# w2 in two rounded parts, fetched from DRAM slot by slot, in a gated cross-attention block with a mixture of experts

## The reference

```python
x = x + tanh(g_xattn) * xattn(layernorm(x), ctx)
h = layernorm(x).reshape(1024, 256)
probs = softmax(30 * tanh(h @ w_gate / 30)); mask = top2(probs)
for e in range(8):
    out += (silu(h @ w1[e]) * (h @ w3[e])) @ w2[e] * (probs * mask)[:, e:e + 1]
x = x + tanh(g_ffn) * out
```

## Time and profile before

| | us |
|---|---|
| median of 3 runs (685.17 to 686.24) | 685.33 |
| the profiled execution's own time | 686.1 |
| its span | 684.3 |
| PE busy | 641.3 (94%) |
| DVE busy | 599.4 (88%) |
| ACT busy | 550.0 (80%) |
| POOL busy | 466.5 (68%) |
| mean DMA traffic over the span | 55 GB/s |

### The profile page before, as it was taken

How to read it: one execution, slowest core, us unless ns; L and a number is a source line. 1 busy time by engine, 2 the same in 40 slices (tenths; PEclk the granted TensorE clock), 3 DMA queues, 4 the chain that set the end, 5 groups by cost and what they waited for, 6 DMA issues and landing times. The chain is left out here.

```text
span 684.3 us, 14974 instructions
## 1 busy us (share of the span) xinstructions
PE 641.3 (94%) x4573; PEld 588.8 (86%) x4574; DVE 599.4 (88%) x1386; ACT 550.0 (80%) x1927; POOL 466.5 (68%) x646
## 2 busy tenths in 40 slices
PE   1789999999999999999999999999998599999994
PEld 0788999999999999999999999999887588888883
DVE  7998899999999999998999999887799887777771
ACT  5898889899988998998899899988886256666660
POOL 4677786688767778777776886788665525565642
PEclk9999999999999999999999999999999589999998
DMA  7203010100020102002010110100089512333232
GB/s 228 62 2 93 2 32 1 40 25 32 2 62 1 32 2 63 32 1 64 1 32 2 55 43 2 61 3 1 1 300 399 172 39 47 47 54 54 46 46 24
DMA packets 35510, 37.73 MB, mean 55 GB/s; under 512 B 2704, under 2 KB 30352, under 8 KB 35440
## 3 DMA queue, kind: packets, MB, share of 16 engines
q1 hardware_dynamic: 31024, 30.84, 13.5%
q0 software_dynamic: 4416, 6.03, 5.5%
HBM read 31.62 MB, written 5.24 MB: 54 GB/s over the span
## 5 line engine op out<-in xcount | busy, mean ns | idle before, releaser
L1518 POOL TENSOR_SCALAR shared<-shared,rsum 128x256 f32<-128x256 f32 x256 | 143.8, 573 | 52.5 <-DVE rsum L1034 47.6
L717 ACT ACTIVATE shared<-s,nmax 128x256 f32<-128x256 f32 x256 | 122.3, 498 | 23.2 <-DVE nmax L1029 23.0
L1512 POOL TENSOR_TENSOR rstd<-rstd,half 128x7 f32<-128x7 f32 (+1 forms) x64 | 87.8, 1371 | 5.3
L1029 DVE TENSOR_REDUCE nmax<-s 128x2 f32<-128x512 f32 x128 | 86.6, 678 | 1.4 <-PE s L380 1.1
L1039 DVE TENSOR_TENSOR pt_lo<-t,pt_hi 128x512 fp32r<-128x512 f32 x124 | 84.1, 679 | 2.3 <-ACT pt_hi L725 1.3
L725 ACT CAST pt_hi<-t 128x512 fp32r<-128x512 f32 x124 | 73.9, 596 | 10.6 <-PE t L395 7.4
L733 ACT ACTIVATE shared<-route_bank,head_w 128x512 f32<-128x512 f32 (+1 forms) x124 | 81.7, 690 | 0.4 <-PE route_bank L409 0.4
L1024 DVE TENSOR_TENSOR qk_lo<-shared,qk_hi 128x512 fp32r<-128x512 f32 x96 | 77.9, 811 | 2.1 <-POOL qk_hi L1529 1.0
L380 PE MATMUL s<-qk_hi 128*128 128x256 f32 x256 | 77.3, 302 | 2.0 <-DVE qk_lo L1024 1.2
L336 PE MATMUL pj_a<-w_ring,xq 128*128 128x256 f32 x488 | 72.2, 291 | 6.3 <-POOL xq L1594 6.3
L395 PE MATMUL t<-ident,shared 128*128 128x128 f32 x496 | 75.0, 274 | 3.0 <-POOL shared L1518 1.7
(11 more groups left out here) (281 smaller groups left out, 1949.1 us busy)
## 6 DMA issues: line engine op xcount, KB each, us to landing
expert_w<-in_w SPq DMA_DIRECT2D x24, 512.0 KB, 9.3
spare<-in_wT SPq DMA_DIRECT2D x19, 256.0 KB, 3.0
wp_raw<-in_wpT SPq DMA_DIRECT2D x16, 256.0 KB, 2.9
spare<-in_wkvT SPq DMA_DIRECT2D x16, 128.0 KB, 3.3
spare<-in_wT SPq DMA_DIRECT2D x9, 128.0 KB, 3.2
spare<-in_x SPq DMA_DIRECT2D x1, 1024.0 KB, 5.9
x_hat<-acc SPq DMA_DIRECT2D x1, 1024.0 KB, 4.6
out<-spare SPq DMA_DIRECT2D x1, 1024.0 KB, 6.9
```

What stands on the lines that cost most here:

```text
L717: e = act.activation(probs[:, st, h * S:(h + 1) * S], s_bank[st][:, h * S:(h + 1) * S], ACT.Exp, bias=nmax[:, st, h:h + 1], accum_out=psum ...
L1029: dve.tensor_reduce(nmax[:, st, :], s_bank[st][:].rearrange("p (h t) -> p h t", h=2), AX, ALU.max, negate=True).then_inc(max_done, 1)
L1512: pool.tensor_tensor(rstd[:, st, c], rstd[:, st, c], half[:, c], ALU.pow).then_inc(rstd_ready, 1)
L1518: m = pool.tensor_scalar(probs[:, st, c], probs[:, st, c], rsum[:, st, h:h + 1], 1.0, ALU.mult, ALU.mult)
```

## The change

In the attention POOL now makes one pair of instructions in every unit: the two parts of one half of the output weights in b = 0 and b = 3, and the two parts of one half of w2 of expert g in b = 1 and b = 2, in the free half of `wp_ring` (`w2_hi`, `w2_lo`). SP loads w2 into `wp_raw` and stores both parts to a DRAM tensor `w2_parts` of 1 MB per expert. The two pairs of the last expert stand among the hand-written last units. Only w1 and w3 are loaded into `expert_w`.

In the experts SP reads the slot's expert number and fetches 1 MB of parts into one half of `w2_ring`, as soon as the down product two slots earlier is done. ACT rounds `hidT`, DVE makes its rest (`hidden_rest`), and the down product is twelve products of rounded operands. PE turns the hidden rows of slot n right after the rows of slot n + 2, ahead of all products of slot n + 1, and ACT copies `hidT` ahead of rounding w1.

```diff
+            def load_w2(e):
+                sp.dma_start(wp_raw[:], w2[e].rearrange("(j p) h -> p j h", p=P)).then_inc(w2_loaded, 16)
+
+            def store_w2(e):
+                sp.wait_ge(w2_split, 2 * (e + 1))
+                sp.dma_start(w2_parts[e].rearrange("i j p h -> p i j h"), wp_ring[:, (e + 1) % 2].bitcast(F32))\
+                    .then_inc(route.w2_stored, 16)
+
+            for g in range(1, 3):
                 sp.wait_ge(w_ready, g)
                 load_w(g)
-                sp.wait_ge(wp_ready, g)
-                load_wp(g)
-            sp.dma_start(route.gate_w[:], w_gate.rearrange("(k p) e -> p k e", p=P)).then_inc(route.gw_loaded, 16)
-            sp.dma_start(route.table[:], tables).then_inc(route.gw_loaded, 16)
-            sp.wait_ge(w_ready, G)
-            sp.dma_start(x1, x.rearrange("b (s p) h -> p (b s) h", p=P)).then_inc(x_reloaded, 16)
-            def load_expert(e, some=(0, 1, 2)):
+            for g in range(G - 1):
+                sp.wait_ge(wp_ready, g + 1)
+                load_w2(g)
+                if 1 <= g < G - 2:
+                    sp.wait_ge(w_ready, g + 2)
+                    load_w(g + 2)
+                if g == G - 2:
+                    sp.dma_start(route.gate_w[:], w_gate.rearrange("(k p) e -> p k e", p=P)).then_inc(route.gw_loaded, 16)
+                    sp.dma_start(route.table[:], tables).then_inc(route.gw_loaded, 16)
+                    sp.wait_ge(w_ready, G)
+                    sp.dma_start(x1, x.rearrange("b (s p) h -> p (b s) h", p=P)).then_inc(x_reloaded, 16)
+                store_w2(g)
+                load_wp(g + 1)
...
+            load_w2(G - 1)
+            def load_expert(e):
...
+                for i in range(2):
+                    sp.dma_start(at[:, i * n:(i + 1) * n].rearrange("p (k c) -> p k c", k=KT),
+                                 (w1, w3)[i][e].rearrange("(k p) c -> p k c", p=P)).then_inc(route.e_loaded, 16)
 
             sp.wait_ge(pj_done, 4 * U)
-            for e in range(E - 1):
+            for e in range(E):
                 load_expert(e)
-            sp.wait_ge(acc_read, 4 * (G - 1))
-            load_expert(E - 1, (0, 1))
-            sp.wait_ge(tile_out, ST)
-            load_expert(E - 1, (2,))
+            store_w2(G - 1)
...
+                    if g > 0:
+                        wait(route.w2_stored, 16 * g)
...
+            def w2_hi(e, a):
+                if a == 0:
+                    pool.wait_ge(w2_loaded, 16 * (e + 1))
+                    if e > 0:
+                        pool.wait_ge(out_done, 4 * e)
+                n = slice(2 * a, 2 * a + 2)
+                pool.tensor_scalar(wp_ring[:, (e + 1) % 2, 0, n], wp_raw[:, n], 1.0, 1.0, ALU.mult, ALU.mult).then_inc(w2_hi_done, 1)
+
+            def w2_lo(e, a):
+                pool.wait_ge(w2_hi_done, 2 * e + a + 1)
+                n = slice(2 * a, 2 * a + 2)
+                pool.tensor_tensor(wp_ring[:, (e + 1) % 2, 1, n], wp_raw[:, n], wp_ring[:, (e + 1) % 2, 0, n].bitcast(F32),
+                                   ALU.subtract).then_inc(w2_split, 1)
...
-                if prep and b >= 2:
-                    wp_hi(g + 1, 1 - par, b - 2)
-                    wp_lo(g + 1, 1 - par, b - 2)
+                if b == 0:
+                    wp_hi(g, par, 1)
+                    wp_lo(g, par, 1)
+                elif b < 3:
+                    w2_hi(g, b - 1)
+                    w2_lo(g, b - 1)
+                elif prep:
+                    wp_hi(g + 1, 1 - par, 0)
+                    wp_lo(g + 1, 1 - par, 0)
...
             widen(28, 0, 1)
+            w2_hi(G - 1, 0)
+            w2_lo(G - 1, 0)
             power(31, 1)
             heads_hi(30, 2, 2)
             scale_probs(29, 1, 1)
+            w2_hi(G - 1, 1)
+            w2_lo(G - 1, 1)
             scale_probs(30, 0, 0)
...
+            def step(n, par):
+                e = sp.value_load(slot_expert[0:1, bass.ds(n, 1)], min_val=0, max_val=E - 1)
+                if least(n, 2):
+                    sp.wait_ge(y_done, n - 1)
+                sp.dma_start(w2_ring[:, par].bitcast(F32),
+                             w2_parts[bass.ds(e, 1)].rearrange("e i j p h -> p (e i) j h")).then_inc(w2_in[par], 16)
+
+            sp.wait_ge(slots_known, 1)
+            sp.wait_ge(route.w2_stored, 16 * E)
+            steps(sp, step)
             sp.wait_ge(scattered, 16 * SLOTS)
...
             def turn_hidden(n, par):
                 pe.wait_ge(hid_ready, n + 1)
                 if least(n, 1):
-                    pe.wait_ge(ht_ready, n)
+                    pe.wait_ge(ht_split, n)
                 for j in range(IT):
                     m = pe.transpose(ht_bank[:, j * P:(j + 1) * P], hid[:, par, j * P:(j + 1) * P], ident[:])
                 m.then_inc(ht_done, 1)
 
             def down(n, par):
-                e = pe.value_load(slot_expert[0:1, bass.ds(n, 1)], min_val=0, max_val=E - 1)
-                pe.wait_ge(ht_ready, n + 1)
+                pe.wait_ge(ht_split, n + 1)
+                pe.wait_ge(w2_in[par], loads(n, par))
                 if least(n, 2):
                     pe.wait_ge(y_copied, n - 1)
-                for j in range(IT):
-                    m = pe.matmul(y_bank[par][:, 0:H], hidT[:, par, j * P:(j + 1) * P],
-                                  w2_sb[:, bass.ds(e, 1), j, :].rearrange("p e i -> p (e i)"), start=j == 0, stop=j == IT - 1)
+                trio = [(j, l, i) for j in range(IT) for l, i in ((hidT, 0), (hidT, 1), (hidT_lo, 0))]
+                for q, (j, l, i) in enumerate(trio):
+                    m = pe.matmul(y_bank[par][:, 0:H], l[:, par, j * P:(j + 1) * P], w2_ring[:, par, i, j],
+                                  start=q == 0, stop=q == len(trio) - 1)
                 m.then_inc(y_done, 1)
...
                     turn_rows(n + 2, par)
                 more = not isinstance(n, int) or n + 1 < SLOTS
+                turn_hidden(n, par)
                 if more:
                     hidden(n + 1, 1 - par, 0)
-                turn_hidden(n, par)
-                if more:
                     hidden(n + 1, 1 - par, 1)
...
-            act.wait_ge(route.e_loaded, 48 * E)
+            act.wait_ge(route.e_loaded, 32 * E)
...
                     rows_turned(n + 2, par)
-                    weights_high(n + 2, par, (0,))
                 act.wait_ge(ht_done, n + 1)
                 if least(n, 2):
                     act.wait_ge(y_done, n - 1)
                 act.copy(hidT[:, par, :], ht_bank[:]).then_inc(ht_ready, 1)
+                if more:
+                    weights_high(n + 2, par, (0,))
                 if not isinstance(n, int) or n + 1 < SLOTS:
                     silu(n + 1, 1 - par)
...
+            def hidden_rest(n, par):
+                dve.wait_ge(ht_ready, n + 1)
+                dve.tensor_tensor(hidT_lo[:, par, :], ht_bank[:], hidT[:, par, :].bitcast(F32), ALU.subtract).then_inc(ht_split, 1)
+
             def step(n, par):
                 more = not isinstance(n, int) or n + 2 < SLOTS
                 if more:
                     rows_rest(n + 2, par)
                     e = expert_of(n + 2)
+                hidden_rest(n, par)
+                if more:
                     weights_rest(n + 2, par, e, 0)
                 if not isinstance(n, int) or n + 1 < SLOTS:
                     take_hidden(n + 1, 1 - par)
```

More of the change, by code:

```diff
@@ L285, in _ @@
             load_wp(0)
-            for g in range(1, G):
+            def load_w2(e):
[5 more added lines that the diff above has]
+            for g in range(1, 3):
                 sp.wait_ge(w_ready, g)
@@ L1785, in experts @@
         hid = sb("hid", [P, 2, I])
-        hidT = sb("hidT", [P, 2, I])
+        hidT = sb("hidT", [P, 2, I], F32R)
         y_sb = sb("y_sb", [P, 2, H])
@@ L2231, in block_kernel @@
     x_hat = nc.dram_tensor("x_hat", [B * S + P, H], F32).ap()
+    w2_parts = nc.dram_tensor("w2_parts", [w2.shape[0], 2, w2.shape[1] // P, P, H], F32).ap()
     T, E = B * S // P, w1.shape[0]
@@ L2259, in block_kernel @@
         attention(nc, x, ctxT, wT, wkvT, wpT, cols, eye, w_gate, tables, firsts, acc, attn_gate, ident, col, half, spare, row_norm,
-                  route, x_hat, out, expert_w, early, w1, w3, w2)
-        experts(nc, expert_w, early, firsts, out, acc, ident, route, x_hat, slots, w1.shape[2])
+                  route, x_hat, out, expert_w, early, w1, w3, w2, w2_parts)
+        experts(nc, expert_w, early, firsts, out, acc, ident, route, x_hat, slots, w1.shape[2], w2_parts)
 def table_columns(experts, slots, rows):
```

27 lines of the change are left out of this document (13 added, 14 removed).

## The result

The changed kernel takes **702.16 us** (median of four, 699.46 to 704.34) beside 685.25 of the kernel before (685.07 to 686.24): slower, ratio 1.0239, 95% interval 1.0223 to 1.0256. The forecast was 682.5 with a range to 690.5, so it was wrong, and by more than its range.

What follows compares the result with a forecast made beforehand. PE was taken to bound the kernel, at 5.18 us per slot. Terms -6.7 + 1.0 + 0.4 + 1.5 + 1.0 = -2.8 us took the profiled 686.1 to 683.3, median 682.5; range 679.3 to 690.5.

Steps and rivals of the forecast that it cites:

- Point 5: Expert slots: fetching w2's parts brings DMA demand to 5.0 of 4.81 us; scatters settle a little later, costing 1.5 us once.
- Point 1: Down product on PE: twelve products of 0.12 us, 1.44 in all, replace eight passes of 1.73; gain 0.29 us per slot.
- Point 2: Transposes on PE: hidden rows turned directly after the row turns save one switch, 0.08 us per slot; period becomes 4.81.
- Point 4: DVE and ACT in the slots: added work fits, but a new loop of 4.83 us closes; cost 0.4 us for all slots.
- Point 3: Opening of the experts: PE waits for slot 0's hidden rows, and DVE's extra work eats early gains; cost 1.0 us.
- Points 6 and 7: POOL's added pairs: hidden in the attention's units, cost 0; in its hand-written tail, cost 1.0 us, bounds 0 and 2.5.
- Point 8: Kernel's end: the last down product waits 0.7 us longer, but the last scatter waits for a landing anyway; cost 0.
- B: Rival, expert slots: the scatter chain becomes the bound, slower than before; 690.5 us, or 696 at worst; chance 0.28.
- d: Extra time per link between scatters beyond 4.64 us; it costs from 0.17, and 0.8 was seen once.
- the ring: Not forecast, named after the measurement: PE waits for a gather, the gather for a scatter ahead, that scatter for a landing.
- D: Rival, expert slots: fetched parts land after over 8 us and PE waits before the down product; about 692 us; chance 0.05.
- A: Rival, whole kernel: nothing new binds, scatters are undisturbed and the tail absorbs its pairs; -5.7 us, 679.6; chance 0.12.

Runs made afterwards that it cites:

- the exchange: The changed kernel with the gather issued ahead of the scatter on POOL's queue: 696.34 us; the same in the kernel before: 686.29 us.
- the hi-only kernel: The changed kernel with only w2's hi half fetched and eight products for twelve: 688.81 us; also with late first fetches and no lo part made: 692.05 us.
- the half fetch: The changed kernel fetching only the hi half of w2's parts (512 KB) from the third slot on, still twelve products: 685.43 us.
- the last version: The changed kernel with w2's hi part alone, no lo part made, late first fetches, and the gather ahead of the scatter: 682.02 us.

## Why the prediction was wrong

**Point 5 failed.** Its demand was somewhat high: fetch 3.4 us and gathers with scatters 1.6 of a slot's engine time, 5.0 in all; in the stretch that runs at 4.87 us the engines' share is 0.89, which is 4.3. What failed is the step that "a slipping scatter moves out from under the fetch", so that the whole would cost 1.5 us once. The runs show a loss that goes on: links of 118.5 us with the whole fetch and 105.4 with half of it, 13 us in place of 1.5. Its own sign of being wrong, a landing over 4.2 us, came true with a median of 4.6 in 572 to 640 us. The step looked only at the scatter and its own chain. A scatter that slips takes the next gather with it, since both stand in one stream on POOL, and PE waits for that gather. That this way counts is shown by the exchange (5.8 us under the whole fetch, 10 in the hi-only kernel, 0 in the kernel before); that the traffic is what starts it, by the smaller fetches (17 us for the second half of the bytes, nothing for the first). Under the whole fetch it is the smaller part of the loss: with the gather first the links still take 115.3 us, and the waits put that down to scatters that land late and hold y_sb. Why the scatters do not move out from under the fetch is not shown by a run; SP's fetch waits for PE's down product, so a late PE makes a late fetch, and in the trace of the hi-only kernel the scatters settle right behind it.

**Point 1** held: 1.42 us for 1.44. Here the Trainium skill's 0.109 us for 256 columns ("TensorE: Matmul & The Clock Gate", section "Back-to-back issue gap") would have made 1.31; the trace has 1.42 / 12 = 0.118. **Point 2** was worth 0.01 us, not 0.08; the period is 4.87, which is 5.18 less point 1's 0.31. **Point 4** held in that its loop did not lengthen the slot beyond that in the good stretch; its 4.83 and PE's 4.87 can't be told apart there. **Points 1 to 4** without the traffic: links of 105.4 us in the half fetch, 5.8 less than before, where 6.7 less some of 0.4 was forecast. So the gain that the forecast is built on was there, and the traffic took it and more.

**Point 3** was too low and missed its cause. PE's own part is small (from first gather to first scatter 18.8 us with the fetches late, 18.2 in the kernel before: 0.6, where 1.0 was forecast). The first two fetches in front of the gathers' landing, which the sum has at nothing, cost 3.2 more: 22.0 us from first gather to first scatter in the changed kernel. The prediction does not ask what SP's queue does in the moment it is let go.

**Points 6 and 7** together were put at 1.0 and cost 2.2 until the first gather. Part of it lies in the units: SP's first load of w1 and w3, behind the last projections, leaves at 499.78 us in place of 498.56, 1.2 us later. That a unit with a pair had once been no longer than one without was too thin a proof: 0.04 us per unit can't be seen between two units, but makes over 1 us in 32. Where the lo part is not made in the attention this load leaves at 498.4 to 498.5 and the first gather comes at 548.2 to 548.3; since those kernels also store only half of the parts, it stays open which of the two costs. In the tail PE stood 1.18 us at 505.60 for the first pair, just above the 0.6 to 1.1 named. (The upper bound in point 7 is added up wrongly: by its own terms the two pairs leave 1.3 + 1.9 = 3.2 uncovered, not 2.5.)

**Point 8** held: 6.0 us from the last scatter to the end, 5.9 before.

**The rivals.** B was nearest: POOL waits for landings (31.6 us over the whole kernel, 12.7 before), and with d = 0.8 it gave 696. With the gather out of the way the links are 5.24 us, so d = 0.60, by which B gives some 692; that the exchange still measures 696.3 is the start, first scatter at 573.4 where B had 567.7. The 5.8 us more of the changed kernel are the ring that B did not have. B had 0.28; with D's 0.05 the two come to more than the 0.31 that the prediction gave to slower in all, but part of B's range (d up to 0.36) is not slower. A's slot was right (the half fetch shows it), with an attention and an opening that ate the gain: 685.4. The sentence on the Trainium skill ("DMA: Bandwidth & Descriptors", section "Queues, rings and completion order") beside B, with 0.5 to 0.9 us ahead of each scatter, is neither confirmed nor excluded: the median landing rose by 0.3, single ones by 3. Longer rows, which by that rule should lie longer in front of a scatter, left its median at 4.1 us where short ones had 4.3 with the gather first (longest 8.0 and 6.3), and at 4.7 where short ones had 4.1 without.

**Left open:** why single scatters take 6 to 7 us; whether the place of the fetch ahead of the scatter decides it, as two traces suggest; why the same kernel stays in the ring in some executions and leaves it in others (changed kernel from 641 us on, long rows 690 or 703, the hi part alone 683 or 696); what sets 4.82 in the last version, where the loop of point 4 (4.83) and the scatter's chain (4.64) are both near. A third buffer of y_sb, and a fetch left out when the slot's expert is that of two slots before, were not tried.

## What to carry to other kernels

When a change adds traffic, work out the engines' share at the period that is hoped for, not at today's, but don't take it for the answer: here up to 0.80 cost at most 1.1 us with twelve products and 0.89 ran undisturbed for 38 us, while the hi-only kernel was in the ring at 0.66. Ask what is in flight at the moment when each transfer that matters is issued, and what stands behind each transfer that can be late in the stream that issues it: a load for the future queued behind a store that waits for a landing can turn a hidden delay into a ring. And when an edit that plainly saves time at one place changes nothing in total, test it in a version in which the suspected ring is open.

## What was not expected of the hardware

- How late a scatter lands does not follow the share of the engines' time: 3.8 us median and 4.0 at most at 0.68, 3.8 and 4.5 at 0.80, 4.1 and 4.5 in a stretch at 0.89, but 4.6 and 6.9 in one at 0.78, and 4.5 and 4.9 at 0.66 (hi-only, 600 to 640 us), where it was issued right behind a fetch.
- A fetch of 1 MB in rows of 8 KB lands after 5.0 us and in rows of 1 KB, with seven times as many packets, after 5.3.
- The issue of a scatter on POOL itself grows under load: 1.58 us, but 2.61 and 2.63 at 596.98 and 610.48, and 2.2 in the median in the ring of the hi-only kernel (600 to 640 us).
- After 3.1 us of idle time at the opening TensorE ran at its lower level until 562.4, and the first twelve products cost 2 us more than in the kernel before (558.23 to 563.3 beside 554.11 to 557.3).
